# Attention with the values as the stationary operand, the softmax sum inside the layer norm's epsilon, and row statistics finished on GpSimd

## The reference

```python
x = x + _layernorm(attn(_layernorm(x), wq, wk, wv, wo))
x = x + _layernorm(ffn(_layernorm(x), norm_w, router_w, w1, w3, w2))

def attn(x, ...):
    q, k, v = x @ wq.T, x @ wk.T, x @ wv.T
    q, k = rope(q), rope(k)
    w = softmax(q @ k.T / sqrt(128))
    return (w @ v) @ wo.T

def _layernorm(x, eps=1e-5):
    return (x - mean(x)) / sqrt(var(x) + eps)
```

## Time and profile before

| | us |
|---|---|
| median of 3 runs | 1219.79 (1219.04 to 1222.67) |
| the profiled execution, time | 1217.32 |
| its span, first to last instruction | 1215.6 |
| TensorE busy | 1048.5 (86%) |
| VectorE busy | 763.4 (63%) |
| ScalarE busy | 593.8 (49%) |
| GpSimd busy | 529.3 (44%) |
| mean granted TensorE clock | 0.955 of full speed |

### The profile page before, as it was taken

The page is one execution under the profiler, slowest core; times in us unless marked ns, Lnnn a source line. Parts: engine busy times, 40 slices in busy tenths (PEclk is TensorE's granted clock), DMA queues, the critical chain, the costliest instruction groups (busy, mean ns, idle before and its releaser), DMA issues.

```text
span 1215.6 us, 25424 instructions
## 1 busy us (share of the span) xinstructions
PE 1048.5 (86%) x7272; PEld 699.7 (58%) x7273; DVE 763.4 (63%) x1817; ACT 593.8 (49%) x1156; POOL 529.3 (44%) x628
## 2 busy tenths in 40 slices
PE   1789996386999849999999999999999999999940
PEld 0456664154676626766666766666766666666620
DVE  3679998588999934447634447635447636635436
ACT  1556664272888923355335455334555333333312
POOL 2311111482588845344444354444354444454415
PEclk9999999696999979999999999999999999999985
DMA  9800000000000023236337535337536337433345
GB/s 331 291 1 0 0 0 1 0 0 5 14 13 17 17 49 83 76 92 152 86 91 171 127 92 153 89 92 168 131 92 148 92 94 188 123 92 86 87 136 162
DMA packets 146302, 110.70 MB, mean 91 GB/s; under 512 B 92592, under 2 KB 132144, under 8 KB 146224
## 3 DMA queue, kind: packets, MB, share of 16 engines
q1 hardware_dynamic: 131248, 68.72, 22.0%
q0 software_dynamic: 14976, 40.91, 11.9%
HBM read 56.11 MB, written 33.03 MB: 73 GB/s over the span
## 4 chain that ended last, share of the span: by engine, by line
PE 59%; DVE 2%; DMA 1%; issue 1%; ACT 0%; POOL 0%; ACTq 0%; SPq 0%; DVEq 0%; POOLq 0%
PE psum_s L1821 34%; PE psum_o L1840 17%; PE psum_s L1829 6%; PE psum_t L532 2%; PE psum_t L1783 1%; DVE arena L1613 1%; DMA arena<-expert_rows 0%; DVE f_stats L1639 0%; DMA arena<-arena 0%; DMA arena<-sorted_rows,token_of_row 0%; DVE arena L1619 0%; DMA expert_rows<-arena,result_row_of_row 0%; PE psum_t L487 0%; DVE f_tmp L334 0%; ACT arena L1598 0%
## 5 line engine op out<-in xcount | busy, mean ns | idle before, releaser
L1821 PE MATMUL psum_s<-w_all,arena 128*128 x1872 | 432.7, 381 | 13.6 <-DMA arena<-arena 12.8
L1488 POOL DMA_INDIRECT expert_rows<-arena,result_row_of_row x156 | 157.7, 1011 | 352.7 <-ACT arena L1573 350.9
L1821 PEld LDWEIGHTS psum_s<-w_all,arena 128*128 128x128 f16 x1872 | 174.3, 98 | 213.2 <-issue 22.9
L1743 DVE SCALAR_TENSOR_TENSOR arena<-psum_s,gate_scale,arena 128x512 f32<-128x512 f32 x156 | 117.1, 751 | 201.9 <-PE psum_s L1821 197.8
L1840 PE MATMUL psum_o<-w_all,arena 128*128 x1872 | 229.9, 273 | 1.5 <-DVE arena L1736 1.5
L1840 PEld LDWEIGHTS psum_o<-w_all,arena 128*128 128x128 f16 x1872 | 181.7, 98 | 47.9 <-issue 3.6
L1736 DVE TENSOR_TENSOR arena<-psum_s,arena 128x512 f16<-128x512 f32 x156 | 107.6, 690 | 148.2 <-ACT arena L1562 147.3
L1573 ACT ACTIVATE arena<-psum_o 128x256 f32<-128x256 f32 x156 | 60.1, 385 | 251.4 <-PE psum_o L1840 251.4
L1479 POOL DMA_INDIRECT arena<-sorted_rows,token_of_row x156 | 153.7, 985 | 55.7 <-issue 45.6
L1567 ACT ACTIVATE arena<-psum_s,silu_scale 128x512 f32<-128x512 f32 x156 | 107.4, 688 | 122.1 <-PE psum_s L1821 122.1
L1562 ACT ACTIVATE arena<-psum_s 128x512 f16<-128x512 f32 x156 | 93.3, 598 | 19.6 <-PE psum_s L1829 13.9
(11 more groups left out here) (223 smaller groups left out, 1311.1 us busy)
## 6 DMA issues: line engine op xcount, KB each, us to landing
w_all<-in_L_ffn_w SPq DMA_DIRECT2D x24, 512.0 KB, 10.5
arena<-expert_rows SPq DMA_DIRECT2D x48, 256.0 KB, 3.4
sorted_rows<-w_all SPq DMA_DIRECT2D x24, 256.0 KB, 2.6
x_sb<-in_L_attn_x SPq DMA_DIRECT2D x4, 1024.0 KB, 8.9
arena<-expert_rows SPq DMA_DIRECT2D x8, 512.0 KB, 5.8
out<-x_sb SPq DMA_DIRECT2D x8, 512.0 KB, 6.6
arena<-sorted_rows,token_of_row POOLq DMA_INDIRECT x156
arena<-arena SPq DMA_TRANSPOSE x156
```

What stands on the lines that cost most here:

```text
L1488: nc.gpsimd.indirect_dma_start(expert_rows[h][:, :], bass.IndirectOffsetOnAxis(ap=targets[:, h, t : t + 1], axis=0), y_row[:, u, :], None) ...
L1743: nc.vector.scalar_tensor_tensor(h_row, psum_b, gate_scale[:, 0:1], silu_a, ALU.mult, ALU.mult).then_inc(s_h, 1)
L1821: last = nc.tensor.matmul(bank, e_xT[:, u, lx * DC + c, :], w_split[:, bass.ds(e * EW + at, FF)], start=(q == 0), stop=(q == 3 * DC - 1))
```

## The change

The values become the stationary operand of the product: for each block of 128 keys three matmuls of 128 columns, whose result in psum_o is already turned (head dimension by token). The turn of o_tok through TensorE goes, and with it o_part and o_tok. The row is no longer divided by its softmax sum. Instead GpSimd computes (s * root_eps) squared per row and adds it to the variance, and also makes the shift from the mean; VectorE's sum, reciprocal, y_var and y_negmean go. The half sums of all tiles are kept (`row_sum` has 2 * NT columns). GpSimd's `split` uses tensor_scalar with a scalar per partition, and its loops are written out in full in place of `pool.Fori`.

```diff
+O_SCALE = 2.0**-24
-        row_sum = take(2)
-        row_rec = take(1)
+        row_sum = take(2 * NT)
+        root_eps = take(1)
+        eps_part = take(1)
...
-            def split(group, done):
-                if not (isinstance(done, int) and done == 0):
-                    pool.wait_ge(s_w_lo, done)
-                raw = w_raw[:, bass.ds(group * GROUP, GROUP)]
-                scale = scale_g[:, :, :].rearrange("p e g -> p (e g)")[:, bass.ds(group, 1)]
-                nc.gpsimd.tensor_tensor(w_tmp, raw, scale.to_broadcast([P, GROUP]), ALU.mult).then_inc(s_w_tmp, 1)
-                pool.wait_ge(s_w_tmp, done + 1)
+            def split(group):
+                if splits_done[0]:
+                    pool.wait_ge(s_w_lo, splits_done[0])
+                splits_done[0] += 1
+                nc.gpsimd.tensor_scalar(w_tmp, w_raw[:, group * GROUP : (group + 1) * GROUP],
+                                        scale_g[:, :, :].rearrange("p e g -> p (e g)")[:, group : group + 1], None,
+                                        ALU.mult).then_inc(s_w_tmp, 1)
+                pool.wait_ge(s_w_tmp, splits_done[0])
                 pool.wait_ge(s_w_hi, group + 1)
...
             def normalise(t, splits):
+                i = t % NT
+                pool.wait_ge(s_exp, 2 * t + 2)
+                if t:
+                    pool.wait_ge(s_yvar, t)
+                nc.gpsimd.tensor_scalar(eps_part, row_sum[:, 2 * i : 2 * i + 1], row_sum[:, 2 * i + 1 : 2 * i + 2],
+                                        root_eps[:, 0:1], ALU.add, ALU.mult).then_inc(s_eps, 1)
+                pool.wait_ge(s_eps, 2 * t + 1)
+                nc.gpsimd.tensor_tensor(eps_part, eps_part, eps_part, ALU.mult).then_inc(s_eps, 1)
+                pool.wait_ge(s_eps, 2 * t + 2)
+                pool.wait_ge(s_ymv, t + 1)
+                nc.gpsimd.tensor_tensor(y_var, eps_part, y_mv[:, 1:2], ALU.add).then_inc(s_yvar, 1)
                 pool.wait_ge(s_yvar, t + 1)
                 nc.gpsimd.tensor_tensor(y_rstd, y_var, neg_half[:, 0:1], ALU.pow).then_inc(s_yrstd, 1)
                 pool.wait_ge(s_yrstd, t + 1)
-                nc.gpsimd.tensor_tensor(y_shift, y_negmean, y_rstd, ALU.mult).then_inc(s_yshift, 1)
+                nc.gpsimd.tensor_scalar(y_shift, y_mv[:, 0:1], y_rstd[:, 0:1], -1.0, ALU.mult, ALU.mult).then_inc(s_yshift, 1)
...
# ScalarE, step
                 if fin:
                     act.wait_ge(s_pv, t - 1)
-                    act.wait_ge(s_rec, t - 1)
-                    nc.scalar.activation(o_part, psum_o[:, HD : 2 * HD], ACT.Copy, scale=row_rec).then_inc(s_o_part, 1)
+                    if norm:
+                        act.wait_ge(s_proj, t - 2)
+                    nc.scalar.activation(oT[:, 0, :], psum_o[:, 0:P], ACT.Copy, scale=O_SCALE).then_inc(s_o_hi, 1)
...
-                if fin:
-                    act.wait_ge(s_to, t - 1)
-                    nc.scalar.activation(oT[:, 0, :], psum_y[:, 0:P], ACT.Copy).then_inc(s_o_hi, 1)
...
# VectorE, step
-                if fin:
-                    dve.wait_ge(s_o_part, t - 1)
-                    if norm:
-                        dve.wait_ge(s_to, t - 2)
-                    nc.vector.scalar_tensor_tensor(o_tok, psum_o[:, 0:HD], row_rec, o_part, ALU.mult,
-                                                   ALU.add).then_inc(s_o, 1)
-                if turn:
-                    dve.wait_ge(s_exp, 2 * t)
-                    nc.vector.tensor_scalar(row_sum[:, 0:1], row_sum[:, 0:1], row_sum[:, 1:2], P_SCALE,
-                                            ALU.add, ALU.mult).then_inc(s_sum, 1)
                 if new:
                     half_max(t, 0)
-                if turn:
-                    dve.wait_ge(s_sum, t)
-                    nc.vector.reciprocal(row_rec, row_sum[:, 0:1]).then_inc(s_rec, 1)
                 if fin:
                     dve.wait_ge(s_o_hi, t - 1)
-                    nc.vector.tensor_tensor(oT[:, 1, :], psum_y[:, 0:P], oT[:, 0, :], ALU.subtract).then_inc(s_o_lo, 1)
+                    nc.vector.scalar_tensor_tensor(oT[:, 1, :], psum_o[:, 0:P], O_SCALE, oT[:, 0, :], ALU.mult,
+                                                   ALU.subtract).then_inc(s_o_lo, 1)
...
                     dve.wait_ge(s_ystat, t - 1)
+                    if norm:
+                        dve.wait_ge(s_yshift, t - 2)
                     dve.sem_inc(s_held, 1)
                     nc.vector.bn_aggr(y_mv, y_stats).then_inc(s_ymv, 1)
-                    dve.wait_ge(s_ymv, t - 1)
-                    nc.vector.tensor_scalar(y_var, y_mv[:, 1:2], attn_eps[:, 0:1], None, ALU.add)
-                    nc.vector.tensor_scalar(y_negmean, y_mv[:, 0:1], -1.0, None, ALU.mult).then_inc(s_yvar, 1)
...
# TensorE, step
-                if fin:
-                    pe.wait_ge(s_o, t - 1)
-                    if norm:
-                        pe.wait_ge(s_ynorm, t - 2)
-                    nc.tensor.transpose(psum_y[:, 0:P], o_tok, ident[:, :]).then_inc(s_to, 1)
...
                     pe.wait_ge(s_o_lo, t - 1)
+                    if norm:
+                        pe.wait_ge(s_ynorm, t - 2)
...
                         at = slice(kc * P, (kc + 1) * P)
-                        nc.tensor.matmul(psum_o[:, 0 : 2 * HD], pT[:, 0, at], v_sb[:, kc * 2 * HD : (kc + 1) * 2 * HD],
-                                         start=(kc == 0), stop=False, skip_group_check=True)
-                        last = nc.tensor.matmul(psum_o[:, 0:HD], pT[:, 1, at], v_tiles[:, kc, 0, :],
-                                                start=False, stop=(kc == NT - 1), skip_group_check=True)
+                        for k, (lv, lp) in enumerate(((0, 0), (0, 1), (1, 0))):
+                            last = nc.tensor.matmul(psum_o[:, 0:P], v_tiles[:, kc, lv, :], pT[:, lp, at],
+                                                    start=(kc == 0 and k == 0), stop=(kc == NT - 1 and k == 2))
```

More of the change, by code:

```diff
@@ L178, in sandwich_kernel @@
         rot = shared.rearrange("p (u m n) -> p u m n", u=2, m=2)
-        o_tok, o_part = shared[:, 0:HD], shared[:, HD : 2 * HD]
-        oT = shared[:, 2 * HD : 2 * HD + P].bitcast(F16).rearrange("p (l t) -> p l t", l=2)
-        y_norm = shared[:, 2 * HD + P : 2 * HD + P + D]
+        oT = shared[:, 0:P].bitcast(F16).rearrange("p (l t) -> p l t", l=2)
+        y_norm = shared[:, P : P + D]
         qk_tok = take(2 * 2 * HD).rearrange("p (u n) -> p u n", u=2)
@@ L201, in sandwich_kernel @@
         y_var = take(1)
-        y_negmean = take(1)
         y_rstd = take(1)
@@ L276, in sandwich_kernel @@
         s_held_p = sem("pool_waits_held")
+        s_eps = sem("row_eps_ready")
         s_yvar = sem("y_var_ready")
@@ L654, in normalise @@
                 if splits is not None:
-                    split(splits + 1, splits + 1 - PAIRS)
+                    split(splits + 1)
             def first_rows(j):
                 pool.wait_ge(s_first_row, j + 1)
-                if not (isinstance(j, int) and j == 0):
+                if j:
                     pool.wait_ge(s_first_st, 16 * j)
@@ L676, in _ @@
                     pool.wait_ge(s_scale_f, 1)
-                rotate(n0)
-                if b:
-                    split(0, 0)
-                    rms_root(pool, 0)
-                with pool.Fori(1, PAIRS) as i:
+                for i in range(PAIRS):
                     rotate(n0 + i)
                     if b:
-                        split(SPLITS * i, i)
+                        split(SPLITS * i)
+                        if i == 0:
+                            rms_root(pool, 0)
                 t0 = b * NT
                 if b == 0:
-                    with pool.Fori(0, NT - 2) as i:
+                    for i in range(NT - 1):
                         normalise(t0 + i, None)
@@ L691, in _ @@
                     first_rows(0)
-                    first_rows(1)
-                    normalise(t0, SPLITS * PAIRS)
-                    with pool.Fori(1, NT - 2) as i:
+                    for i in range(NT - 1):
                         first_rows(i + 1)
-                        normalise(t0 + i, SPLITS * (PAIRS + i))
-                    first_rows(NT - 1)
-                normalise(t0 + NT - 2, None)
+                        normalise(t0 + i, SPLITS * (PAIRS + i) if i < NT - 2 else None)
                 if b == 0:
@@ L911, in _ @@
             link(nc.vector.tensor_tensor(attn_eps[:, :], scale_a[:, 2:3], scale_a[:, 3:4], ALU.mult))
-            link(nc.vector.tensor_scalar(attn_eps[:, :], attn_eps[:, :], X_SCALE * QKV_SCALE, None, ALU.mult))
-            link(nc.vector.tensor_tensor(attn_eps[:, :], attn_eps[:, :], attn_eps[:, :], ALU.mult))
-            nc.vector.tensor_scalar(attn_eps[:, :], attn_eps[:, :], LN_EPS, None, ALU.mult).then_inc(s_scale_a, 1)
+            nc.vector.tensor_scalar(root_eps, attn_eps[:, :], X_SCALE * QKV_SCALE * P_SCALE * O_SCALE * float(np.sqrt(LN_EPS)), None,
+                                    ALU.mult).then_inc(s_scale_a, 1)
             dve.wait_ge(s_wt_hi, 4)
```

(3 more changed lines are left out.)

21 lines of the change are left out of this document (7 added, 14 removed).

## The result

The changed kernel takes 1224.28 us (median of 15 runs, 1220.53 to 1227.71) against 1219.79 for the kernel before (15 runs, 1218.0 to 1223.33). The ratio is 1.0034, with a 95% interval of 1.0021 to 1.0047: slower by some 4.5 us, where 1207 us was forecast. The two profiled executions have spans of 1222.4 and 1215.6 us, 6.8 apart, at nearly the same clock (0.954 and 0.955).

The account below looks back on a forecast made before the run. VectorE bounds batch 0's step; in batch 1 VectorE is full but held, and GpSimd with ScalarE becomes the bound. Terms -10.3 - 1.0 + 1.0 - 1.1 - 1.0 = -12.4 take 1217.3 to 1204.9, plus 2.5: 1207 us, range 1203 to 1211.

Parts of the forecast that it names:

- the split's tensor_scalar: GpSimd's split: first instruction 0.79 us where the tensor_tensor took 1.04; with constant indices, second split's step 0.53 us shorter.
- rival B: GpSimd binds harder: large tensor_scalar 1.04, small ones 0.5, ring 8.92, 1215 us; or projections lose, 1212; chance 0.15.
- the ring: Batch 1's steady step: GpSimd and ScalarE waiting on each other from y_norm to next y_norm, 7.80 us becoming 8.27.
- Batch 0: First batch's attention: VectorE sets the step, 8.24 us falling to 7.52; -10.3 us over its steps.
- drain: End of batch 0's attention: turn, o_hi's and o_lo's hand-overs leave a serial chain, -1.0 us (bounds 0 and 1.5).
- behind the all-reduce: Between the batches: GpSimd's added row statistics have nothing to hide them, +1.0 us (0.4 to 1.5).
- projections: Batch 1's projections: VectorE's held L1069 shortens with the split's L638, half let through, -1.0 us (0 to -1.8).
- +5 the other way: Batch 1's projections: +5 us if GpSimd's L641 gets ahead of VectorE's next two-input instruction, 0.7 a pair.
- The end of attention: End of batch 1's attention: the same three hand-overs as in batch 0's drain go, -1.1 us.
- A: GpSimd does not bind: large tensor_scalar near 0.61, small ones 0.19, ring 7.87, 1200 to 1202 us; chance 0.2.
- C: Product with the values: stationary loads don't fit under 128 columns, slower once a pair exceeds 0.071 us; 1247; chance 0.04.
- D: No gain in batch 0: TensorE's wait for the last p_lo replaces VectorE's lines, 1216 to 1218 us; chance 0.04.

Follow-up runs that it names:

- two_ops: The changed kernel with a second operation (times 1.0) added to the split's tensor_scalar on GpSimd; 1210.22 us, ratio 0.9919 to the kernel before.
- before_unrolled: The kernel before with only GpSimd's loops written out, all instructions unchanged; 1218.79 us, ratio 0.9995.
- split_tt: The changed kernel with the split's first instruction on GpSimd a broadcast tensor_tensor again; 1214.30 us, ratio 0.9968 to the kernel before.
- two_ops_hoist: two_ops, with the next tile's epsilon made inside the first split, ahead of its wait for split_hi; 1198.29 us, ratio 0.9846 to the kernel before.
- before_ts: before_unrolled with the split's first instruction as the one-operation tensor_scalar of the changed kernel; 1218.19 us, ratio 0.9998 to the kernel before.

## Why the prediction was wrong, step by step

**The step that failed** is the price of the split's tensor_scalar: 0.79 us as twice a one-input copy, between bounds of 0.61 and 1.04. It takes 1.58, outside both. The upper bound was put as "no gain", as if a simpler instruction could not cost more than the tensor_tensor that it replaces; no row of before showed a tensor_scalar of that size on GpSimd. The only one, L618 with 16 columns and also one operation, cost 0.300 against 0.192 for the copy of its width. The prediction used that 0.1 us for the small instructions and in rival B, and in the split's price not at all.

The Trainium skill, page "GPSIMD Engine Reference", section "Engine selection", calls GpSimd's one-input work roughly line-rate. The copy's 0.62 us and the two-operation form's 0.70 lie near each other here; by that rule, the trace disagrees for the form with one operation, 1.50 to 1.65 us.

Batch 1's step shows the error term by term. All are differences of starts, before in the earlier trace rows, after in the rows above.

| part of the ring | before | forecast | after | two_ops |
|---|---|---|---|---|
| y_norm to the first split's L641 / L640 | 1.46 | 1.46 | 1.59 | 1.32 |
| to the second split's first instruction | 1.81 | 1.81 | 1.82 | 1.83 |
| to its second instruction | 1.40 | 0.87 | 1.65 | 0.77 |
| to the statistics | 2.21 | 2.21 | 2.25 | 2.26 |
| statistics, to the next y_norm | 0.92 | 1.92 | 1.94 | 1.91 |
| sum | 7.80 | 8.27 | 9.25 | 8.09 |

Of the 0.98 us between forecast and measurement, 0.78 is the second split. 0.13 is the first: it ends after ScalarE's high part now, so the wait for split_hi, behind which its price was to be hidden, is gone and the price itself stands in the ring. The statistics, priced at 1.00, measured 1.02. With a tensor_scalar of 0.70 us the ring closes at 8.09, where the forecast's own sum gives 8.18, and the time is 1210.2, 3 us over the forecast. So the ring was right up to the length at which GpSimd's stream has no wait left. One duration in it was not, and past that length the first split's price counts too, which the ring left out.

**Batch 0** was right in mechanism and a little large in size: the step went to 7.68, forecast 7.52, with VectorE as the bound. What was taken off was 0.38 + 0.07 as forecast. From bn_stats to the weight maximum it takes 158.60 - 157.70 = 0.90 us, where 1.02 - 0.33 = 0.69 was forecast: bn_aggr starts 0.65 behind bn_stats, with 0.23 of wait, where it started 0.57 behind it before, and is followed by the maximum after 0.25, not 0.12. The scalar_tensor_tensor L1028 costs no more than L1040 did (0.19 from start to start in both traces). So the gain over batch 0's marks was 8.2 us, not about 10.3.

**Between the batches** the forecast was -1.0 (drain -1.0, behind the all-reduce +1.0, projections -1.0), measured -0.13. By the starts in the two traces the drain, from the last mark to the all-reduce, was right: 17.70 to 16.66 us, -1.04. The gap behind the all-reduce was 0.41 shorter, without a forecast. The middle term stands in GpSimd's timeline, which answers to the earlier trace rows:

```profile
211.29 0.34 POOL L649 TENSOR_SCALAR arena<-arena 128x1 f32<-128x1 f32 x1 [7.13 <-issue]
...
212.25 0.60 POOL L657 TENSOR_TENSOR arena<-arena,neg_half 128x1 f32<-128x1 f32 x1
...
213.89 0.72 POOL L663 TENSOR_TENSOR x_sb<-x_sb,arena 128x256 f32<-128x256 f32 x1 [0.68 <-ACT arena L785]
```

Before, the residual was this one:

```profile
220.43 0.72 POOL L653 TENSOR_TENSOR x_sb<-x_sb,arena 128x256 f32<-128x256 f32 x1 [0.68 <-ACT arena L780]
```

From the first statistic to the residual it is 2.60 us; before, the pow at 218.89 was followed by it 1.54 later. That is +1.06 for +1.0. The projections, forecast at -1.0, measured +0.25 (from row_root to the first mark, 71.93 to 72.18). Their steady pairs got 0.16 shorter (5.51 to 5.35 us), as forecast, since VectorE's L1057 is held less (1.28 us for 1.63), though L635 is longer; but an early pair got 0.56 longer (6.08 for 5.52). The steady pair answers to the earlier trace rows:

```profile
255.50 1.28 DVE L1057 TENSOR_SCALAR arena<-x_sb,f_mean,f_rstd 128x256 f32 x2
255.91 1.60 POOL L635 TENSOR_SCALAR arena<-w_all,scale_g 128x512 f32<-128x512 f32 x1
```

The bound "+5 the other way" of the prediction, that GpSimd's L641 gets ahead of VectorE's two-input instruction, was a real danger, and the long tensor_scalar is what kept it off: VectorE's L972 takes 0.74 us here, and 1.72 in before_unrolled (as L968), in split_tt and in two_ops, whose steady pairs are 6.11, 6.10 and 5.77 us apart. The form that costs most in the query tiles costs least in the projections.

**The end of attention** was forecast at -1.1 and cost +4.9: GpSimd's last tiles go through the same stream, with L635 at 419.49, 422.97, 428.74 and 432.21, and everything behind the residuals starts late. In two_ops_hoist this stretch is 1.4 us shorter than before.

**The start** (+2.0) had no place in the forecast, and nothing shows that it is the change's. The first mark of the kernels with the changed statistics lies at 69.1 to 75.1 us in nine profiled executions (mean 72.2), in the three with the old ones at 70.3 to 73.3 (mean 71.4). Without it the profiles differ by 4.8 us, as the medians do by 4.5.

The sum: -12.4 forecast; +8.2 in batch 1's steps, +6.0 at its end, +2.1 in batch 0, +0.9 between (of it +1.25 in the projections) and +2.0 of the start make 19.2; -12.4 + 19.2 = +6.8, as measured.

**The rivals.** B, GpSimd binds harder, named the right engine, but it put the large tensor_scalar at 1.04 and hence the ring at 8.92 and the time at 1212 to 1215; at that price the ring was 8.44 and the time 1214.3 (split_tt). A is refuted by the same rows: GpSimd binds. C, the loads under 128 columns, is refuted by 0.056 us a pair, far from the 0.071 at which it decides. The Trainium skill, page "TensorE: Matmul & The Clock Gate", section "Back-to-back issue gap", gives about 81 ns for such pairs; the trace still disagrees. D is refuted by batch 0's 7.68. That it could be slower through GpSimd itself was not among the rivals, and slower by any way had 0.05, because the price's upper bound was closed by an argument and not by a row.

## What to carry to other kernels

An instruction that the trace doesn't show in its form and size has no upper bound in "it does less than the one it replaces": leave it open upward, and ask at which price the sign turns (here, on a line between 1214.3 us at 1.04 and 1224.3 at 1.58, an instruction of about 1.3 us). A form is part of the price: before moving work, time each spelling of the same operation once, since here the longer formula was the faster one, and do it in each stage: the same instruction that filled GpSimd's stream in one stage kept GpSimd out of VectorE's way in another. And count an engine's whole stream, not only the ring through its waits: once the stream is as long as the step, nothing is hidden in a wait any more, and small instructions cost their full price in each step.

## What the runs showed of the hardware that was not expected

GpSimd's tensor_scalar of 128x512 f32 takes 1.50 to 1.65 us in the mean with one operation, and with two 0.69 us in the median (up to 1.13 in the projections), the same operands and result; with 256 columns and one operation it is 0.94 to 0.97. Why the shorter formula is slower, no run shows.

VectorE's mark is held while GpSimd works on certain instructions. With two operations, in two_ops_hoist, the mark at 368.61 ends when L635 does (368.41 + 0.70 = 369.11):

```profile
368.61 0.50 DVE L1043 SCALAR_TENSOR_TENSOR arena<-arena,neg_alpha 128x1 f32<-128x1 f32 x1
```

```profile
368.41 0.70 POOL L635 TENSOR_SCALAR arena<-w_all,scale_g 128x512 f32<-128x512 f32 x1
```

With one operation, in before_ts, the mark at 388.62 ends at 389.17, while GpSimd's L639 runs from 388.48 to 390.04:

```profile
388.62 0.55 DVE L1041 SCALAR_TENSOR_TENSOR arena<-arena,neg_alpha 128x1 f32<-128x1 f32 x1
```

```profile
388.48 1.56 POOL L639 TENSOR_SCALAR arena<-w_all,scale_g 128x512 f32<-128x512 f32 x1
```

So the mark was held for the first 0.69 us of L639 and not for the other 0.87. The Trainium skill, page "SBUF — State Buffer", section "Terms", says of the port pair shared by the two engines that it is held for the full instruction. By that rule, the trace agrees for the form with two operations and disagrees for the one with one; that the extra 0.87 us is a stretch in which GpSimd doesn't use the port is only argued from these two ends.
